# One ones-matmul group for two units: VectorE sums pairs of softmax weight tiles in the graph attention of a GNN stack

## The chip, the cores and the metric

The kernel runs on one core of a Trainium2 chip. The metric is the device time of one execution, in microseconds. Kernels are compared by medians of several executions.

## What is computed

A stack of four graph layers on 3125 nodes of 256 features with 50000 edges, each with a residual: a GIN layer with two batch norms, a GCN layer with two convolutions, a normalised sum over neighbours, and a two-level graph attention (GAT). The change lies in the attention's first level, which has four heads:

```python
h = (x @ W).reshape(N, H, C)
al_s = jnp.einsum('nhc,hc->nh', h, a_src)
al_d = jnp.einsum('nhc,hc->nh', h, a_dst)
e = jax.nn.leaky_relu(al_s[src] + al_d[dst], NEG_SLOPE)
m = jax.ops.segment_max(e, dst, num_segments=N)
ex = jnp.exp(e - m[dst])
denom = jax.ops.segment_sum(ex, dst, num_segments=N)
alpha = ex / denom[dst]
out = jax.ops.segment_sum(h[src] * alpha[:, :, None], dst, num_segments=N)
```

The kernel holds the edges as a dense matrix of counts `ct_d`, source nodes by destination nodes. For a head, `ex` is then a dense matrix of weights, zero where there is no edge. `out` is the feature rows times this matrix, and `denom` are its column sums.

## The kernel before

Nodes come in 25 blocks of Q = 125 (`NB = 25`). Destination nodes are split into two halves of 13 and 12 blocks (`HALF`, `COLS` = 1625 and 1500 columns). A step k of the attention is one head and one half: steps 0 to 7 are the four heads of the first level, k even the half of 13 blocks, k odd that of 12; steps 8 and 9 are the second level. A step has 25 units, one for each block j of source nodes; q = 25 k + j numbers the units.

One unit passes through the engines like this:

- SyncE loads the unit's counts into one of six buffers (`LC`).
- VectorE, `score` (L2458): the logits of the unit into the tile `TT[q % TR]`, one of a ring of TR = 4 tiles in R. It waits until TensorE has finished unit q - 4 (`l3_pe`) and until a DMA that reads the same tile has landed (`den_sum`).
- ScalarE, `exp_unit` (L1667): the exponential in place.
- VectorE, `weights` (L2471): times the counts, in place, then `l3_t` is raised. Ahead of it, in steps 0 to 5, one `max_unit` for the next head (L2242, for j = 0 L2239).
- TensorE, `unit` (L1402): waits for `l3_t`, then multiplies the features of the block with the weights, two groups of 128 features by the chunks of 500 columns (and one of 125), accumulating over the 25 units in PSUM banks 0 to 6. An fp32 matmul shows as two instructions in the trace: a unit of 13 blocks has 16, one of 12 blocks 12.
- The denominators of steps 0 to 5 (`DPE` = 6) are made in two parts. The first 1000 columns: TensorE, four matmuls of 250 columns against a block of ones, into four groups of 32 partitions of bank 6 (L1409, eight instructions a unit). The rest, 625 or 500 columns: POOL adds the tile's end to a DRAM tensor with accumulating DMAs (`den_sum`, L884), one chain for even and one for odd units. In steps 6 to 9 VectorE adds whole tiles instead (`den_add`, L2434) and there are no ones matmuls.

VectorE's order is written out in `attention`: score(q + 2), then den_add(q - 1) where there is one, then weights(q) with its maximum, then `beside(q)`. That is `results_in(q)` in steps 0 to 7: small results of the step before. TensorE makes one of them after each unit from j = 2 on (`result`): the transposed column maxima (L1302, L1309), the denominators (L1342, L1347), rows of their inverses (L1356) and the projections by W31 (L1366); a step of 13 blocks leaves 18 results, one of 12 leaves 14. VectorE reads them two units of its own later (j - 2 - LATER): L2330 to L2348, L2376 and L2377, L2387, L2397 with L2400. All go through PSUM bank 7: `aux_bank` lets TensorE write result i + 1 only after `aux_free` says that VectorE has read result i. In step 0 there is `late_max` as well: six more maxima, beside units 0, 1, 3, 5, 7 and 9 (`HELD`, L2242 on wA).

At the end of a step ScalarE takes the sums out of PSUM (`evac_step`, L1680, L1686).

`PT` is a buffer of 2000 columns; from column 1000 on it holds the second part of the denominators (`den_back`) and `denQ`. `denB` lies in wB and serves as denominators in steps 7 and 9.

Of the kernel before, what the change touches and what calls it, by code (L numbers as in the profile page):

```python
# [5 lines left out]
ALU = mybir.AluOpType  # L6
# [11 lines left out]
Q = 125  # L18
NB = N // Q
# [67 lines left out]
TR = 4  # L87
# [43 lines left out]
def gnn_stack(nc, x, src, dst, edge_weight, eps0, W01, b01, g01, be01, W02, b02, g02, be02,  # L131
              W11, b11, W12, b12, Wl1, bl1, root_idx, W2, b2, W31, as31, ad31, b31, gnw, gnb, gnms,
              W32, as32, ad32, b32, out):
    with ExitStack() as ctx:
        sems = {}

        def S(name):
            if name not in sems:
                sems[name] = ctx.enter_context(nc.semaphore(name))
            return sems[name]  # L140

        def sb(name, shape, dt=F32):
            return ctx.enter_context(nc.sbuf_tensor(name, shape, dt))
# [26 lines left out]
        PT = sb("PT", [128, 4 * 4 * Q])  # L170
# [41 lines left out]
        TT = [R[:, s * LW:(s + 1) * LW] for s in range(TR)]  # L212
# [18 lines left out]
        denB = wB[:, CT * NYC * 6:CT * NYC * 6 + COLS[1]]  # L231
# [102 lines left out]
        def lc_at(q):  # L334

            return MET + q + sum(a < q for a in HELD)
# [99 lines left out]
        for g_ in range(len(CB) + 1):  # L436
            if g_ < len(CB):
                HW_SEQ += [("turn", g_, k) for k in range(KT)]
            if g_:
                j, nj = CB[g_ - 1]  # L440
# [15 lines left out]
        def bank_of(f, c):  # L456
            return (f * 3 + c, 0) if c < 3 else (6, f * Q)
# [16 lines left out]
        PRE = [len(MGROUPS[0]) + 1, len(MGROUPS[1]) + 1]  # L474
# [11 lines left out]
        DPE = STEPS - 2  # L486
# [6 lines left out]
        def sum_count(q):  # L493

            k, j = divmod(q, NB)
            return (NB // 2 if j % 2 else NB - NB // 2) * k + j // 2
        denQ = PT[:, LW:LW + 3 * Q]

        def den_span(k):

            return (0, 0) if k < DPE else (0, COLS[k % 2])

        def den_adds(q):

            k, j = divmod(q, NB)
            return sum(NB for i in range(k) if den_span(i)[1]) + (j if k < STEPS + 2 and den_span(k)[1] else 0)


        EVS = [7, 6]
        ev0 = [sum(EVS[i % 2] for i in range(k)) for k in range(STEPS + 3)]  # L510
# [410 lines left out]
        def _(pe):  # L921
# [95 lines left out]
            for n, (what, g, x_) in enumerate(HW_SEQ):  # L1017
                j, nj = CB[g]
# [3 lines left out]
                else:  # L1022
                    done = HW_SEQ.index(("turn", g, KT - 1)) + 1
                    pe.wait_ge(S("ring_ev"), base["hw"] + done)
                    for m in range(hw_blocks(g, x_)):
                        o = (x_ + m - j) * Q
                        for k in range(KT):
                            last = mm(ps[0:Q, n % 4, m * D:(m + 1) * D], HT[:, g % 2, k, o:o + Q], w01[:, k, :],
                                      start=k == 0, stop=k == KT - 1)
# [216 lines left out]
            for q in range(LAYERS * NB):  # L1246
                step_unit(q)
                k, j = divmod(q, NB)
# [140 lines left out]
            def unit(q, rows):  # L1389
                k, j = divmod(q, NB)  # L1390
                half = k % 2
                pe.wait_ge(S("l3_t"), q + 1)
                for f in range(KT):
                    for c, (o, w) in enumerate(CHUNKS[half]):
                        bank, at = bank_of(f, c)
                        if j == 0 and k not in (0, STEPS) and bank < 6:
                            pe.wait_ge(S("agg_ev"), ev0[k - 1] + bank + 1)
                        if j == 0 and bank == 6 and f == 0 and 0 < k <= DPE:
                            pe.wait_ge(S("den_out"), k)
                        if j == 0 and bank == 6 and f == 0:  # L1400
                            pe.wait_ge(S("aux_free"), PRE[0] if k == 0 else aux0[k - 1] if k < STEPS else pre2 + PRE[0])
                        last = mm(ps[:, bank, at:at + w], rows[0:Q, j, f * 128:(f + 1) * 128], TT[q % TR][0:Q, o:o + w],  # L1402
                                  start=j == 0 and at == 0, stop=j == NB - 1, skip_group_check=c == 3)
                if k < DPE:
                    if j == 0 and k:
                        pe.wait_ge(S("den_out"), k)
                    nb, first, at = DQ[half]
                    for c in range(4):
                        last = mm(ps[c * 32:(c + 1) * 32, 6, at:at + nb * Q], ones[0:Q, 0:32],  # L1409
                                  TT[q % TR][0:Q, c * nb * Q:(c + 1) * nb * Q],  # L1410
                                  start=j == 0 and first == 1, stop=j == NB - 1, skip_group_check=True)
                last.then_inc(S("l3_pe"), 1)

            pe.wait_ge(S("ln_done"), 4 * NB + HALF[0][1])
# [21 lines left out]
            n = 0  # L1436
# [295 lines left out]
        def _(dve):  # L1732
            v_ = nc.vector
            tt, ts, stt, cp = v_.tensor_tensor, v_.tensor_scalar, v_.scalar_tensor_tensor, v_.tensor_copy
# [158 lines left out]
            for i, (g, part) in enumerate(PUNITS):  # L1893
                j0, nb = PG[g]
# [8 lines left out]
                for c, (o, w) in enumerate(LCHUNKS):  # L1903
                    for k in range(KT):
                        n = 4 * i + c * KT + k
# [330 lines left out]
            def max_unit(t, dst, score, first, done, name):  # L2236

                if first:
                    ts(dst, t, score, None, ALU.min).then_inc(S(name), 1)  # L2239
                else:  # L2240
                    dve.wait_ge(S(name), done)
                    stt(dst, t, score, dst, ALU.min, ALU.max).then_inc(S(name), 1)  # L2242
# [7 lines left out]
            for q in range(LAYERS * NB):  # L2250
                k, j = divmod(q, NB)
# [190 lines left out]
            def score(q):  # L2442

                k, j = divmod(q, NB)
                half, w = k % 2, COLS[k % 2]
                u = UV[k // STEPS][half]
                s8 = asc[0:Q, 1, (k // 2) * NB + j:(k // 2) * NB + j + 1] if k < STEPS else asb[0:Q, 1, j:j + 1]
                if q == 0:
                    dve.wait_ge(S("rows_clear"), 1)
                if q >= TR:  # L2450
                    dve.wait_ge(S("l3_pe"), q - TR + 1)
                    if q - TR < DPE * NB:
                        dve.wait_ge(S(f"den_sum{(q - TR) % NB % 2}"), 16 * (sum_count(q - TR) + 1))
                    if den_adds(q - TR + 1):
                        dve.wait_ge(S("l3_den"), den_adds(q - TR + 1))
                if j == 0:
                    dve.wait_ge(S(f"uv_in{half}"), 16 * (k // 2 + 1))
                stt(TT[q % TR][0:Q, 0:w], u[0:Q, 0:w], s8, u[0:Q, w:2 * w], ALU.add, ALU.max).then_inc(S("l3_a"), 1)  # L2458

            def weights(q):  # L2460

                k, j = divmod(q, NB)
                half, w = k % 2, COLS[k % 2]
                r = lc_at(q)
                t, lc = TT[q % TR][0:Q, 0:w], LC[r % LCR][0:Q, 0:w]
                dve.wait_ge(S(f"lc_in{r % LCR}"), 16 * (r // LCR + 1))
                if k < STEPS - 2:
                    max_unit(lc, macc[half][0:Q, :], asc[0:Q, 0, (k // 2 + 1) * NB + j:(k // 2 + 1) * NB + j + 1],
                             j == 0, len(EARLY) + lc_at(q - 1) + 1, "l3_max")
                dve.wait_ge(S("l3_exp"), q + 1)  # L2470
                stt(t, t, 1.0, lc, ALU.min, ALU.mult).then_inc(S("l3_t"), 1)  # L2471

            def attention(q0, q1, beside):

                score(q0)
                score(q0 + 1)
                for q in range(q0, q1):
                    if q + 2 < q1:
                        score(q + 2)
                    if q > q0:  # L2480
                        den_add(q - 1)
                    weights(q)
                    beside(q)
                den_add(q1 - 1)

# [27 lines left out]
            def norm_vectors(t0, t1, n):  # L2513
# [19 lines left out]
                tt(f[3], w[2], f[4], ALU.subtract).then_inc(S("gn_aff"), 1)  # L2533

            attention(0, STEPS * NB, results_in)
            norm_vectors(0, GT, 0)
            for i in range(results(STEPS - 1)):
# [80 lines left out]
```

## Time and profile before

| | us |
|---|---|
| median of 3 runs | 3499.51 |
| lowest, highest | 3499.39, 3502.76 |
| profiled execution | 3490.76 |
| its span | 3488.7 |
| TensorE busy | 3178.3 |
| VectorE busy | 2430.9 |
| L1402, TensorE, B features, x2800 | 1094.9 |
| L2471, VectorE, x250 | 444.8 |
| L2458, VectorE, first level, x200 | 368.9 |

The profile is of one execution. Times of groups are sums of durations; matmuls overlap, so that the starts of neighbouring ones say more than their durations. "Idle before" is the time in which the engine had nothing to do ahead of an instruction, and the releaser is what ended it.

### The profile page before, as it was taken

Reading aid. Unit: us, or ns where it says so; the run is one execution under the profiler, and the core shown is the slowest. Engines: PE = TensorE matmul, PEld = TensorE weight load, DVE = VectorE, ACT = ScalarE, POOL = GpSimd, SP = SyncE. Lnnn points to the kernel's source line nnn. Section 1 sums busy time; section 2 is a strip of 40 time slices with the busy share of each in tenths; the row PEclk is TensorE's granted clock in tenths of the full one; section 3 lists DMA queues with packets and bytes.
Section 4 is the critical chain, followed back from the end, with each engine's and each line's share of the span. In section 5 each row is a group of like instructions: output and inputs, shape, how many; then the busy total and the mean of one; then the engine's idle time right before and its main releaser. Section 6 shows DMA issues by size and latency. Waiting matters only on the chain.

```text
span 3488.7 us, 34571 instructions
## 1 busy us (share of the span) xinstructions
PE 3178.3 (91%) x12587; PEld 1842.6 (53%) x12587; DVE 2430.9 (70%) x3261; ACT 859.4 (25%) x1133; POOL 834.7 (24%) x710
## 2 busy tenths in 40 slices
PE   5679986987999999999499999999999999996998
PEld 4567764764545455587344444444444444473444
DVE  9972322346356553246898888888888898888987
ACT  1013322335000001143222222222222222252322
POOL 7888888840000000011011112211111000020000
PEclk6559998998999999999699999999999999998999
DMA  9999997993555553545466557655555422283422
GB/s 324 364 327 289 309 264 199 297 250 97 185 174 173 179 178 120 175 153 165 149 163 143 133 124 153 136 128 125 135 118 128 108 88 69 85 315 124 129 62 68
DMA packets 290916, 602.34 MB, mean 173 GB/s; under 512 B 94028, under 2 KB 161168, under 8 KB 288699
## 3 DMA queue, kind: packets, MB, share of 16 engines
q1 hardware_dynamic: 147995, 452.89, 40.4%
q0 software_dynamic: 90272, 87.23, 14.7%
q10 hardware_dynamic: 52480, 60.01, 5.8%
q8 instruction: 100, 1.64, 0.2%
q14 instruction: 69, 0.57, 0.0%
HBM read 385.57 MB, written 214.46 MB: 172 GB/s over the span
## 4 chain that ended last, share of the span: by engine, by line
PE 63%; DMA 10%; issue 9%; DVE 9%; POOL 6%; POOLq 2%; ACT 1%; ACTq 0%; DVEq 0%; SPq 0%
PE ps L1402 31%; PE ps L1234 15%; DMA pairs<-w 8%; POOL pairs L828 6%; PE ps L1203 4%; PE ps L1366 3%; PE ps L1409 2%; PE ps L1431 2%; DVE R L2471 2%; PE ps L1151 2%; DVE wB L2434 1%; PE ps L1045 1%; DVE PT L2242 1%; POOLq L818 1%; POOLq L813 1%
## 5 line engine op out<-in xcount | busy, mean ns | idle before, releaser
L1402 PE MATMUL ps<-R,B 125*128 125x500 f32 x2800 | 1094.9, 542 | 24.2 <-DVE R L2471 18.2
L1402 PEld LDWEIGHTS ps<-R,B 125*128 125x128 f32 x2800 | 504.1, 190 | 587.7 <-issue 552.8
L828 POOL DMA_INDIRECT pairs<-w x392 | 605.6, 1545 | 130.2 <-issue 105.7
L1667 ACT ACTIVATE R<-R,asc 125x1625 f32<-125x1625 f32 (+1 forms) x200 | 320.2, 1601 | 959.0 <-DVE R L2458 959.0
L2458 DVE SCALAR_TENSOR_TENSOR R<-H,asc 125x1625 f32<-125x1625 f32 (+1 forms) x200 | 368.9, 1845 | 133.8 <-PE ps L1409 110.6
L2471 DVE SCALAR_TENSOR_TENSOR R<-R 125x1625 f32<-125x1625 f32 (+1 forms) x250 | 444.8, 1779 | 0.0
L1045 PE MATMUL ps<-R,H 125*128 125x375 f32 (+1 forms) x1000 | 299.7, 446 | 51.0 <-DMA R<-pairs 50.5
L884 POOL DMA_DIRECT2D den_d<-R x138 | 118.3, 858 | 771.0 <-DVE R L2471 742.2
L1402 PE MATMUL ps<-R,H 125*128 125x500 f32 (+1 forms) x700 | 274.0, 547 | 19.2 <-DVE R L2471 17.5
L1234 PE MATMUL ps<-R,H 125*128 125x500 f32 (+1 forms) x700 | 275.0, 545 | 10.3 <-ACT H L1524 7.6
L1910 DVE TENSOR_TENSOR Fb<-Fb,ps 128x250 f32<-128x250 f32 (+1 forms) x140 | 67.2, 480 | 307.2 <-PE ps L1045 245.3
L1234 PE MATMUL ps<-R,B 125*128 125x500 f32 (+1 forms) x700 | 268.9, 540 | 1.6 <-ACT R L1608 0.9
L2242 DVE SCALAR_TENSOR_TENSOR Fb<-R,asc,Fb 125x1625 f32<-125x1625 uint16 (+1 forms) x144 | 265.0, 1840 | 0.0
L1045 PEld LDWEIGHTS ps<-R,H 125*128 125x128 f32 x1000 | 184.5, 192 | 126.4 <-DMA R<-pairs 51.1
L1402 PEld LDWEIGHTS ps<-R,H 125*128 125x128 f32 x700 | 125.9, 192 | 160.8 <-issue 131.2
L1234 PEld LDWEIGHTS ps<-R,H 125*128 125x128 f32 x700 | 127.8, 192 | 146.1 <-issue 141.6
L1234 PEld LDWEIGHTS ps<-R,B 125*128 125x128 f32 x700 | 126.0, 190 | 137.0 <-issue 136.1
L1065 PE MATMUL ps<-ident,R 125*125 125x125 f32 x1250 | 170.1, 284 | 22.2 <-ACT B L1564 14.2
L1791 DVE SCALAR_TENSOR_TENSOR R<-ps,Fb,R 128x512 bf16<-128x512 f32 (+3 forms) x392 | 190.1, 543 | 0.0
L1065 PEld LDWEIGHTS ps<-ident,R 125*125 125x125 f32 x1250 | 160.5, 195 | 42.6 <-ACT B L1564 18.9
L849 POOL DMA_DIRECT2D high_d<-Br x13 | 7.8, 601 | 640.5 <-DVEq L2173 640.3
L2097 DVE TENSOR_REDUCE R<-R 125x1 f32<-125x1625 uint16 (+1 forms) x50 | 88.9, 1778 | 101.3 <-DMA R<-ct_d 99.7
(370 smaller groups left out, 3437.4 us busy)
## 6 DMA issues: line engine op xcount, KB each, us to landing
pairs<-R SPq DMA_DIRECT2D x25, 3200.0 KB, 18.3
R<-ct_d SPq DMA_DIRECT2D x187, 406.2 KB, 3.6
R<-ct_d SPq DMA_DIRECT2D x187, 375.0 KB, 3.2
R<-pairs SPq DMA_DIRECT2D x25, 2500.0 KB, 11.7
R<-wt_d SPq DMA_DIRECT2D x50, 812.5 KB, 4.4
R<-wt_d SPq DMA_DIRECT2D x50, 750.0 KB, 4.2
den_d<-R POOLq DMA_DIRECT2D x75, 312.5 KB, 5.7
den_d<-R POOLq DMA_DIRECT2D x75, 250.0 KB, 4.7
```

What stands on the lines that cost most here:

```text
L828: pool.indirect_dma_start(pairs, bass.IndirectOffsetOnAxis(ap=key_u[:, c:c + 1], axis=0), val[:, c, :], None, compute_op=ALU.add)\
L884: pool.dma_start(den_d[a][k % 2], TT[q % TR][:, 8 * Q:w], accum_op=ALU.add).then_inc(S(f"den_sum{a}"), 16)
L1045: last = mm(ps[:, n % 4, 0:w], H[0:Q, j0 + m, k * 128:(k + 1) * 128], pair_rows_at(i)[0:Q, m, o:o + w, 0], start=m == 0, stop=m == nb - 1 ...
L1065: last = tr(ps[0:Q, 4 + 2 * (n % 2) + t, m * Q:(m + 1) * Q], pair_rows_at(i)[0:Q, m, b * Q:(b + 1) * Q, t], ident[0:Q, 0:Q])
L1203: last = mm(ps[:, bank, at:at + w], part[0:rows, jj, f * 128:(f + 1) * 128], TLr[u % TS][0:rows, o:o + w], start=j == 0 and i == 0 and at ...
L1234: last = mm(ps[:, bank, at:at + w], rows[0:Q, j, f * 128:(f + 1) * 128], TL[q % TS][0:Q, o:o + w], start=j == 0 and at == 0, stop=j == NB ...
L1402: last = mm(ps[:, bank, at:at + w], rows[0:Q, j, f * 128:(f + 1) * 128], TT[q % TR][0:Q, o:o + w], start=j == 0 and at == 0, stop=j == NB ...
L1667: a(t, t, ACT.Exp, bias=s2).then_inc(S("l3_exp"), 1)
L1791: stt(TW[c][:, b * CW + lo:(b + 1) * CW], ps[0:EP, (t % 2) * 2 + b, lo:CW], k, TRI[:, 0:CW - lo], ALU.is_equal, ALU.mult, accum_out=later[ ...
L2242: stt(dst, t, score, dst, ALU.min, ALU.max).then_inc(S(name), 1)
L2458: stt(TT[q % TR][0:Q, 0:w], u[0:Q, 0:w], s8, u[0:Q, w:2 * w], ALU.add, ALU.max).then_inc(S("l3_a"), 1)
L2471: stt(t, t, 1.0, lc, ALU.min, ALU.mult).then_inc(S("l3_t"), 1)
```

## The change

In steps 0 to 5 VectorE adds the weight tiles of units q - 1 and q, for every odd j, over the first 1000 columns, after weights(q) and ahead of `beside(q)`: `pair_sum`. The sum goes alternately into the first 1000 columns of PT and of denB (`PAIR`), and `l3_pair` is raised. TensorE leaves out the ones matmuls in even units, and in odd ones runs them on the sum, after the products and a wait for `l3_pair`. The last unit of a step, j = 24, has no partner and is summed alone as before. `pair_sums(q)` is the number of sums up to unit q. `pair_sum` waits for its own engine's weights (`l3_t`), for TensorE to have finished unit q - 4 (`l3_pe`), and once for the first five small results. `score` waits in addition for the sums that read the tile which it overwrites. The wait for `den_out` at the start of a step moves from j = 0 to j = 1. POOL's part of the denominators is unchanged.

```diff
--- before.py
+++ after.py
@@ -506,6 +506,13 @@
             return sum(NB for i in range(k) if den_span(i)[1]) + (j if k < STEPS + 2 and den_span(k)[1] else 0)
 
 
+        PAIR = [PT[:, 0:8 * Q], denB[:, 0:8 * Q]]
+
+        def pair_sums(q):
+
+            k, j = divmod(q, NB)
+            return min(k, DPE) * (NB // 2) + (min((j + 1) // 2, NB // 2) if k < DPE else 0)
+
         EVS = [7, 6]
         ev0 = [sum(EVS[i % 2] for i in range(k)) for k in range(STEPS + 3)]
 
@@ -1401,14 +1408,17 @@
                             pe.wait_ge(S("aux_free"), PRE[0] if k == 0 else aux0[k - 1] if k < STEPS else pre2 + PRE[0])
                         last = mm(ps[:, bank, at:at + w], rows[0:Q, j, f * 128:(f + 1) * 128], TT[q % TR][0:Q, o:o + w],
                                   start=j == 0 and at == 0, stop=j == NB - 1, skip_group_check=c == 3)
-                if k < DPE:
-                    if j == 0 and k:
+                if k < DPE and (j % 2 or j == NB - 1):
+                    if j == 1 and k:
                         pe.wait_ge(S("den_out"), k)
                     nb, first, at = DQ[half]
+                    if j % 2:
+                        pe.wait_ge(S("l3_pair"), pair_sums(q))
+                    t = PAIR[pair_sums(q) % 2] if j % 2 else TT[q % TR]
                     for c in range(4):
                         last = mm(ps[c * 32:(c + 1) * 32, 6, at:at + nb * Q], ones[0:Q, 0:32],
-                                  TT[q % TR][0:Q, c * nb * Q:(c + 1) * nb * Q],
-                                  start=j == 0 and first == 1, stop=j == NB - 1, skip_group_check=True)
+                                  t[0:Q, c * nb * Q:(c + 1) * nb * Q],
+                                  start=j == 1 and first == 1, stop=j == NB - 1, skip_group_check=True)
                 last.then_inc(S("l3_pe"), 1)
 
             pe.wait_ge(S("ln_done"), 4 * NB + HALF[0][1])
@@ -2451,6 +2461,8 @@
                     dve.wait_ge(S("l3_pe"), q - TR + 1)
                     if q - TR < DPE * NB:
                         dve.wait_ge(S(f"den_sum{(q - TR) % NB % 2}"), 16 * (sum_count(q - TR) + 1))
+                    if pair_sums(min(q - TR + 1, DPE * NB - 1)):
+                        dve.wait_ge(S("l3_pair"), pair_sums(min(q - TR + 1, DPE * NB - 1)))
                     if den_adds(q - TR + 1):
                         dve.wait_ge(S("l3_den"), den_adds(q - TR + 1))
                 if j == 0:
@@ -2470,6 +2482,20 @@
                 dve.wait_ge(S("l3_exp"), q + 1)
                 stt(t, t, 1.0, lc, ALU.min, ALU.mult).then_inc(S("l3_t"), 1)
 
+            def pair_sum(q):
+
+                k, j = divmod(q, NB)
+                if k >= DPE or j % 2 == 0:
+                    return
+                n = pair_sums(q)
+                if q >= 4:
+                    dve.wait_ge(S("l3_pe"), q - 3)
+                dve.wait_ge(S("l3_t"), q + 1)
+                if n == 1:
+                    dve.wait_ge(S("aux_full"), PRE[0])
+                tt(PAIR[n % 2][0:Q, :], TT[(q - 1) % TR][0:Q, 0:8 * Q], TT[q % TR][0:Q, 0:8 * Q], ALU.add)\
+                    .then_inc(S("l3_pair"), 1)
+
             def attention(q0, q1, beside):
 
                 score(q0)
@@ -2480,6 +2506,7 @@
                     if q > q0:
                         den_add(q - 1)
                     weights(q)
+                    pair_sum(q)
                     beside(q)
                 den_add(q1 - 1)
```

## Rows read from the trace of the kernel before

**Rows 1.** The page, parts 1 and 4: busy time; chain that ended last
```profile
PE 3178.3 (91%) x12587; PEld 1842.6 (53%) x12587; DVE 2430.9 (70%) x3261; ACT 859.4 (25%) x1133; POOL 834.7 (24%) x710
...
PE 63%; DMA 10%; issue 9%; DVE 9%; POOL 6%; POOLq 2%; ACT 1%; ACTq 0%; DVEq 0%; SPq 0%
```

**Rows 2.** Windows by step: length, busy by engine, then clock, DMA share, GB/s
```profile
1750.98:1914.00 163.02, 160.21 (x614) 76.16 (x614) 148.91 (x91) 41.69 (x27) 21.33 (x26) 0.98 0.66 158
1914.00:2075.36 161.36, 159.85 (x572) 68.16 (x572) 141.19 (x108) 42.38 (x34) 23.02 (x28) 1.00 0.54 124
...
sum 989.62, PE 979.29 PEld 444.34 DVE 868.20 ACT 256.96 POOL 155.14; mean PE 163.22 PEld 74.06 DVE 144.70 ACT 42.83 POOL 25.86
```

**Rows 3.** Waits of VectorE, 1750 to 2741: total us, times, longest us
```profile
DVE R L2458 <- PE ps L1409: 110.6, 133, 2.1
DVE R L2458 <- DMA den_d<-R: 3.0, 3, 1.6
```

**Rows 4.** Timeline of VectorE, a plain unit of 13 blocks: start, duration, instruction
```profile
2202.25 1.91 DVE L2458 SCALAR_TENSOR_TENSOR R<-H,asc 125x1625 f32<-125x1625 f32 x1 [0.75 <-PE ps L1409]
2204.08 1.91 DVE L2242 SCALAR_TENSOR_TENSOR Fb<-R,asc,Fb 125x1625 f32<-125x1625 uint16 x1
```

**Rows 5.** Chain that ended last, two plain units: start, us, what
```profile
2201.62 0.56 PE ps L1409 x8
2202.18 5.67 PE ps L1402 x16
...
2051.38 5.24 PE ps L1402 x12
```

**Rows 6.** Start of step 0: window, timeline of VectorE and TensorE
```profile
1750.98:1817.10 66.12, 65.11 (x240) 30.49 (x240) 64.57 (x37) 16.51 (x10) 7.97 (x10) 0.96 0.66 165
...
1771.49 1.77 DVE L2242 SCALAR_TENSOR_TENSOR wA<-R,asc,wA 125x1500 f32<-125x1500 uint16 x1
1773.18 1.90 DVE L2458 SCALAR_TENSOR_TENSOR R<-H,asc 125x1625 f32<-125x1625 f32 x1
...
1778.59 1.90 DVE L2458 SCALAR_TENSOR_TENSOR R<-H,asc 125x1625 f32<-125x1625 f32 x1
...
1817.10 1.10 PE L1402 MATMUL ps<-R,B 125*128 125x500 f32 x2 [0.58 <-DVE R L2471]
```

**Rows 7.** A denominator row of step 1: timeline of VectorE, chain
```profile
1969.77 1.78 DVE L2458 SCALAR_TENSOR_TENSOR R<-H,asc 125x1500 f32<-125x1500 f32 x1 [1.82 <-PE ps L1409]
...
1974.79 0.67 DVE L2387 COPY wA<-ps 128x500 f32<-128x500 f32 x1
...
1975.88 0.57 PE ps L1356 x4
```

**Rows 8.** A projection of step 1: timeline of VectorE, chain
```profile
2006.64 0.67 DVE L2397 TENSOR_TENSOR Fb<-ps,wA 128x500 f32<-128x500 f32 x1
2007.45 0.68 DVE L2400 BATCH_NORM_STATS2 wB<-Fb 128x6 f32<-128x500 f32 x1
...
2009.02 1.87 PE ps L1366 x4
```

**Rows 9.** Waits of TensorE's weight loads, 1750 to 2741: total us, times, longest
```profile
PEld ps L1302 <- DVE mcol L2330: 6.0, 15, 0.4
```

**Rows 10.** Timeline of TensorE, plain units of steps 6 and 7
```profile
2845.84 50.61 PE L1402 MATMUL ps<-R,B 125*128 125x500 f32 x144
...
3001.64 41.30 PE L1402 MATMUL ps<-R,B 125*128 125x500 f32 x96 [0.16 <-DVE R L2471]
```

**Rows 11.** Line L2434, VectorE: durations in ns min/median/max, first and last start
```profile
L2434 DVE TENSOR_TENSOR wB<-wB,R x48: 1708/1714/1722, 2904.2 to 3459.7; 125x1500 f32<-125x1500 f32 x48
L2434 DVE TENSOR_TENSOR X<-X,R x24: 1842/1844/1847, 2748.3 to 2892.5; 125x1625 f32<-125x1625 f32 x24
```

**Rows 12.** Timeline of VectorE, operations that wait for each other, step 3
```profile
2288.16 0.29 DVE L2336 TENSOR_SCALAR mcol<-mcol,kb 125x13 f32<-125x13 f32 x1
2288.49 0.18 DVE L2337 TENSOR_TENSOR mcol<-mcol,ald 125x13 f32<-125x13 f32 x1
```

## The prediction

> **What bounds the kernel now.** I read the page first. TensorE is busy for 91% of the span, VectorE for 70%, and the chain that ended last is TensorE's for 63% [rows 1]. The change lies in steps 0 to 5 of the heads, so I cut these from the trace: six stretches, 1750.98 to 2740.60, 989.6 us together; in them TensorE is busy 98 to 99% at a granted clock of 0.98 to 1.00, VectorE 88% [rows 2]. (Steps 0 and 1 and the sum of the six stand there; 3 and 5 are like 1, while 2 and 4 have some 172 us.). The waits of VectorE say how the two are coupled: its score (L2458) waits 110.6 us in 133 pieces for TensorE's L1409, and next to nothing else [rows 3]. VectorE is thus the follower, by some 0.75 us a unit, the time that it waits ahead of a plain score [rows 4]. A plain unit of 13 blocks takes TensorE 5.68 us for the products and 0.56 us for the ones matmuls, 6.24 together, and one of 12 blocks 5.24 and 0.56, 5.80 together [rows 5]. The granted clock of nearly 1 is the level of 2.4 GHz.
>
> Two places are tighter than this. The first is the start of step 0, where VectorE has six more maxima to take (L2242 on wA, in the units of HELD). There it has no idle time ahead of its scores, and TensorE waits for it [rows 6]. The second is the hand-over of the small results. They all go through bank 7, and TensorE may write result i+1 only when VectorE has read result i (`aux_free`). With a denominator row of a 12-block step, VectorE's copy ends at 1974.79 + 0.67 = 1975.46, and TensorE goes to the next row at 1975.88 [rows 7]: 0.42 us of play. With a projection the product ends at 2006.64 + 0.67 = 2007.31 and TensorE comes at 2009.02: 1.71 us [rows 8]. That TensorE's weight loads wait for such a read already, 15 times for the maxima (L1302), never over 0.4 us, says that this play is nearly used up [rows 9].
>
> **What the change removes.** 12 of 25 units in each of 6 steps lose their four ones matmuls: 72. The row says 0.56 us each; but step 6, which has none, does nine plain 13-block units back to back in 50.61 us, 5.62 each, and step 7 eight 12-block ones in 41.30, 5.16 each [rows 10]. So what goes is 6.24 - 5.62 = 0.62 and, with 5.20 for the short unit (between this 5.16 and the 5.24 of above), 0.60. Together 36 x 0.62 + 36 x 0.60 = 44 us of TensorE's work. The group's mean of 386 ns is not the price: eight such instructions lie within 0.56 us.
>
> **What it adds.** 72 sums of 1000 columns on VectorE. The same addition takes 1844 ns for 1625 columns and 1714 for 1500, 1.04 ns a column; from either it is 1194 for 1000 [rows 11]. It adds the unit's own weights, just written, and waits for them (`l3_t`). Between operations that don't wait for each other the next starts some 0.08 us before the former's end: scores of 1.91 us are followed 1.83 us later [rows 4]. Here this overlap is lost, and a gap comes on top. A waiting operation starts 0.04 us after the end of the one before (2288.16 + 0.29 to 2288.49), or 0.14 with a semaphore instruction in between (2006.64 + 0.67 to 2007.45) [rows 8, 12]. I take 0.05, nearest to the first, since nothing but waits is between. One sum thus costs 0.08 + 0.05 + 1.194 - 0.08 (the operation behind it overlaps) = 1.24 us; its bounds are 1.11 (nothing exposed) and 1.33 (a gap of 0.14). 72 of them are 89 us, beside 110.6 us of idle time. By totals they fit. Pair by pair they don't.
>
> The Trainium skill, in VectorE: DVE Perf Modes, section The DRAIN you can't avoid, says that the pipe empties after every operation in any case and that a semaphore costs nothing extra. The rows show the contrary: an operation of 1.91 us is followed 0.08 before its end where nothing waits, and one of 0.29 us 0.04 after its end where something does. By that rule of the Trainium skill the sum would cost the lower bound, 1.11; what that gives is a rival below.
>
> The other edits cost nothing. The wait for `l3_pe` at q-3 is one that the score of two units on has made already. TensorE's wait for `l3_pair` stands behind 5.68 or 5.24 us of products that start when the weights are ready, and the sum is there 1.24 us after them. The two buffers are reused four units later, the waits in `score` for sums that VectorE issued earlier itself are past. The accumulating DMAs of POOL (L884) cost VectorE 3.0 us in all [rows 3]; their room, from weights to the score four units on, becomes 5.4 + 1.24 = 6.7 us instead of 6.2 (6.3 instead of 5.8 in the short steps), so they gain some. Queued behind the sum on VectorE are the next score, which has its 0.75 us, and `beside(q)`, the reading of a result, which has 0.42.
>
> **The sum.** I walk the 150 units with three rules. VectorE starts score(q+2) when it is free and TensorE has ended unit q-2 (0.1 us later), then does the maximum, the weights, in odd units the sum, and the result; a 13-block unit is 5.41 us of it (score to score, 1773.18 to 1778.59) and a 12-block one 5.02 (score to copy, 1969.77 to 1974.79) [rows 6, 7]. TensorE starts unit q 0.05 us after its weights, and result i+1 0.05 us after result i was read. Durations are those above. For the kernel before the walk gives 161.9, 161.3, 171.1, 161.3, 171.1, 161.3 for the six steps, 988.0 in all; the trace has 163.0 and 161.4 for the first two and 989.6 in all [rows 2]. With the change:
> - Step 0, first ten units: VectorE needs 10 x 5.41, six maxima of 1.69 (1771.49 to 1773.18 [rows 6]) and 5 x 1.24, 70.4 us; the walk had 65.5 (trace: 66.1 [rows 6]). +5.0. The next four +0.1.
> - Plain pairs: VectorE 2 x 5.41 + 1.24 = 12.06 against 12.48 before (TensorE would be 11.86). -0.42 each; in a short step 11.28 against 11.60, -0.32. VectorE is now the later one. The last eleven units of step 0 give -1.7, the last nine of steps 2 and 4 -1.8 each.
> - Pairs with denominator rows: VectorE reads 1.24 us later, TensorE comes 0.60 earlier, play 0.42: TensorE waits some 1.5 us at bank 7, and the pair takes about 0.9 longer. The column maxima, the inverse and the first rows of a short step come to +0.7 +1.2 +0.6, those of steps 2 and 4 to +0.6 +0.5 +0.9.
> - Pairs with projections: 1.24 + 0.60 - 1.71, some 0.2 us of wait. In the middle of the run -0.35 a pair, but the first pays +0.9; six units come to +0.2 (short) and +0.1 (long).
> - First pair of a step -0.6 (units before it ran ahead); last units of a short step -0.3 and +0.1.
>
> By step: +3.3; +2.0 three times in 1, 3, 5; -0.3 twice in 2 and 4. Together 3.3 + 6.0 - 0.6 = +8.7 us: all 44 us of TensorE's savings are given back, and somewhat more. Steps 6 and 7 and what follows don't change. The profiled execution took 3490.76 us (span 3488.7), which becomes 3499.5; the median of the runs was 8.75 above it, 3499.51, and becomes 3508.2. With the bounds of a sum, 1.11 and 1.33, the walk gives -0.1 and +15.0; an error of 0.04 us in TensorE's saving per unit moves it by 3.5.
>
> **Rivals.**
> 1. Nothing is exposed between weights and sum (1.11 us each). Then VectorE's pace is 11.93 a plain long pair and the waits at bank 7 are 0.13 shorter; the walk gives -0.1 us, 3499.4. (That is how the rule of the Trainium skill, VectorE: DVE Perf Modes, The DRAIN you can't avoid, would have it.) Against it stand the chains of [rows 12]. 0.15; what lies between it and my case, below +7, has another 0.18.
> 2. The result hand-over isn't a constraint, since the reads have more play than the two places show; then only VectorE's own pace counts. The walk without that rule gives +3.3 in step 0, -2.4 in each short and -5.0 in each long step: -13.9, 3485.6. For it speaks that no wait at this place is now over 0.4; against it that there are 15 [rows 9], and the code's wait. It decides by the play at the read: over 1.8 us and the rival holds. 0.08.
> 3. The totals hold: 89 us go into 110.6 us of idle time, and all 44 us of TensorE come off: 3455.5. A ring of four tiles (TR) would have to carry 1.24 us from odd to even units and through the result stretches; in plain pairs alone VectorE's 12.06 is above 11.86. 0.03.
> 4. The short pauses of TensorE lower its granted clock. In step 0's first 66 us it had such pauses, one of 0.58 us, at 0.96 [rows 6], and the steps as they are run at 0.98 to 1.00 [rows 2], so I don't expect it; a twentieth of step 0 at half clock would be +8 us more, inside my upper end.
>
> **How the numbers follow.** Slower is the forecast, with 0.56 for the case of the sum from +7 up: 3508 us. The range 3494 to 3517 has the exposed and unexposed sum with the saving's error at both ends and half of rival 2. A change of 0.2% (7 us) is about what a measurement of this kernel can tell from none. Faster than that: rivals 2 and 3, 0.11. Within: 0.15 + 0.18 = 0.33. Slower: 0.56.
>
> **What would show it.** VectorE's new group at L2496 or thereabouts, 72 of 1194 ns, starting some 0.05 us after the end of the weights; L1409 with 624 instead of 1200 instructions; the wait of L2458 for L1409 down from 110.6 to below 40; TensorE waiting for L2387, L2330 and L2397 for some tens of us in all, pieces of up to 1.5 us; the first ten units of step 0 at about 70.5 us instead of 66.1. I am wrong if the steps 1, 3, 5 are below 161, or if TensorE's waits at results stay small.

## The result, and the profile after

The changed kernel takes 3519.9 us in the median of its runs (3518.8 to 3525.0), against 3499.5 us for the kernel before in the same session: the ratio is 1.0062, with a 95% interval of 1.0051 to 1.0074. It is 20.4 us slower, beyond the upper end of the range, 3517. The profile is that of the run of 3519.42 us.

The page of the changed kernel, parts 1 and 5: busy time by engine, and the scores' group with its count, busy time, mean ns and the idle time ahead of it.

```profile
PE 3152.6 (90%) x12011; PEld 1840.0 (52%) x12011; DVE 2510.8 (71%) x3333; ACT 859.5 (24%) x1133; POOL 834.6 (24%) x710
...
L2470 DVE SCALAR_TENSOR_TENSOR R<-H,asc 125x1625 f32<-125x1625 f32 (+1 forms) x200 | 368.4, 1843 | 68.2 <-PE ps L1419 40.5
```

The sums, from the groups of VectorE by line and shape, 1740 to 3090 us, with the same columns:

```profile
L2496 DVE TENSOR_TENSOR PT<-R 125x1000 f32<-125x1000 f32 x36 | 43.2, 1201 | 4.0 <-DVE R L2483 0.5
```

TensorE has 576 instructions fewer than in [rows 1], 72 times 8; VectorE has 72 more. So the change does what it says. Its windows by step, cut at ScalarE's first eviction of each step as in [rows 2]: length, busy time of TensorE, its weight loads, VectorE, ScalarE and POOL, then clock, DMA share, GB/s.

```profile
1756.91:1924.12 167.21, 152.54 (x517) 73.67 (x517) 161.92 (x102) 40.96 (x26) 20.73 (x25) 0.98 0.64 154
1924.12:2090.60 166.48, 154.88 (x475) 67.14 (x475) 154.66 (x119) 42.37 (x33) 22.48 (x28) 0.99 0.52 120
2090.60:2262.86 172.26, 162.67 (x563) 79.56 (x563) 161.74 (x113) 44.08 (x32) 45.49 (x53) 1.00 0.69 146
...
sum 1010.29, PE 942.35 PEld 434.24 DVE 948.41 ACT 256.23 POOL 155.45; mean PE 157.06 PEld 72.37 DVE 158.07 ACT 42.70 POOL 25.91
```

The six steps take 1010.3 us instead of 989 (the two first windows of before end 0.7 us off an eviction; cut at the evictions they are 162.3, 161.4, 171.3, 161.4, 171.3 and 161.4, 988.9 in all). The steps gained 4.9, 5.1, 1.0, 4.8, 1.0 and 4.6 us, 21.4 together: the whole of the difference between the medians. The two profiled executions differ by more, 28.7 us, and 5.9 of it lies ahead of step 0, which begins at 1756.91 instead of 1750.98 us, in code that the change doesn't touch. TensorE's busy time fell from 979.3 to 942.4, by 37 us, and still it took longer: it waits. VectorE's waits for the ones matmuls fell from 110.6 to 40.5 us; in their place TensorE waits for VectorE. The waits of VectorE and of TensorE's matmuls between 1750 and 2768 us: total, times, longest.

```profile
DVE R L2470 <- PE ps L1419: 40.5, 39, 2.4
...
PE ps L1409 <- DVE R L2483: 38.6, 25, 17.9
PE ps L1309 <- DVE mcol L2340: 12.3, 12, 1.2
PE ps L1316 <- DVEq L2351: 9.0, 6, 2.6
PE ps L1363 <- DVE wA L2397: 7.4, 5, 1.5
PE ps L1373 <- DVE wA L2397: 7.2, 5, 1.5
```

The first of TensorE's lines holds 17.9 us ahead of the first unit, which the kernel before has too (16.8); what is left of it is mostly step 0. There the first ten units take 70.6 us (1756.91 to 1827.48), where the prediction had about 70.5. The other four are the hand-over of small results. Of such waits the kernel before had only one kind at its matmuls, ahead of its L1309 (L1316 of the changed kernel), 4.3 us in 6, longest 0.7; at its weight loads none was over 0.4 us [rows 9]. Here is one, a denominator row of step 1, in VectorE's timeline (start, duration, instruction, idle time ahead of it and what ended it):

```profile
1993.42 1.71 DVE L2483 SCALAR_TENSOR_TENSOR R<-R 125x1500 f32<-125x1500 f32 x1
1995.24 1.20 DVE L2496 TENSOR_TENSOR PT<-R 125x1000 f32<-125x1000 f32 x1
1996.35 0.67 DVE L2397 COPY wA<-ps 128x500 f32<-128x500 f32 x1
```

and in TensorE's:

```profile
1990.37 5.21 PE L1409 MATMUL ps<-R,B 125*128 125x500 f32 x12
1997.08 0.64 PE L1363 MATMUL ps<-ident,dcol 125*128 125x125 f32 x4 [1.50 <-DVE wA L2397]
```

TensorE comes 0.6 us sooner, since the even unit has no ones matmuls, and finds bank 7 unread, since the sum stands ahead of the copy. This is the 1.5 us that the prediction had worked out from [rows 7].

Three things were not in it. The first two are about the sum itself. A sum at the start of step 0, a later one behind which a score follows, and the weights ahead of each, from VectorE's timeline:

```profile
1775.84 1.84 DVE L2483 SCALAR_TENSOR_TENSOR R<-R 125x1625 f32<-125x1625 f32 x1
1777.72 1.20 DVE L2496 TENSOR_TENSOR PT<-R 125x1000 f32<-125x1000 f32 x1
...
2223.23 1.85 DVE L2483 SCALAR_TENSOR_TENSOR R<-R 125x1625 f32<-125x1625 f32 x1
2225.18 1.20 DVE L2496 TENSOR_TENSOR PT<-R 125x1000 f32<-125x1000 f32 x1
2226.52 1.91 DVE L2470 SCALAR_TENSOR_TENSOR R<-H,asc 125x1625 f32<-125x1625 f32 x1
```

The first starts 0.04 us after the weights' end (1775.84 + 1.84), the second, which waits for `l3_pe` as well, 0.10 (2223.23 + 1.85). And the score starts 0.14 us after the sum's end, where a small result starts 0.09 before it (1995.24 + 1.20 to 1996.35 above). So in a plain pair a sum costs not 1.24 but 2226.52 - 2223.23 = 3.29 us less the 1.77 from weights to score without it, 1.52 us.

The third is the clock. The last column maxima of step 1 and the unit behind them, timeline of TensorE:

```profile
1969.21 0.27 PE L1316 MATMUL ps<-ident,uvc 125*26 125x125 f32 x1 [2.58 <-DVEq L2351]
1969.32 6.89 PE L1409 MATMUL ps<-R,B 125*128 125x500 f32 x12
```

Two windows, up to the pause's end and behind it, with the clock as the third number from the right:

```profile
1961.22:1969.21 7.99, 5.42 (x17) 2.33 (x14) 7.41 (x10) 1.55 (x1) 0.84 (x1) 1.00 0.56 126
1969.21:1976.14 6.93, 6.93 (x14) 2.83 (x14) 5.29 (x4) 1.54 (x1) 0.85 (x1) 0.75 0.29 46
```

TensorE waited 2.58 us for the five small operations behind the sum and the last maxima. The unit after the pause took 6.89 us instead of 5.2, at a mean granted clock of 0.75: half of that window at 1.2 GHz, half at 2.4. Below, this is called a stretch at half clock. The same stands in steps 3 and 5, and nowhere in steps 1 to 5 of the kernel before. That is 1.7 us three times.

### The profile page after: what moved, and what is told of

Read it like the earlier page. It is cut to its first block and busy times, and to the rows that moved or that the text cites. A ratio compares the mean times of both kernels' runs of the same rounds, so it can differ in the third digit from the quotient of the medians.

```text
span 3517.3 us, 33578 instructions
## 1 busy us (share of the span) xinstructions
PE 3152.6 (90%) x12011; PEld 1840.0 (52%) x12011; DVE 2510.8 (71%) x3333; ACT 859.5 (24%) x1133; POOL 834.6 (24%) x710
## 5 line engine op out<-in xcount | busy, mean ns | idle before, releaser
L2470 DVE SCALAR_TENSOR_TENSOR R<-H,asc 125x1625 f32<-125x1625 f32 (+1 forms) x200 | 368.4, 1843 | 68.2 <-PE ps L1419 40.5
L1409 PEld LDWEIGHTS ps<-R,H 125*128 125x128 f32 x700 | 126.2, 192 | 160.9 <-issue 131.4
L1072 PE MATMUL ps<-ident,R 125*125 125x125 f32 x1250 | 172.7, 287 | 27.6 <-ACT B L1574 16.3
```

Source lines behind the costliest of these rows:

```text
L1072: last = tr(ps[0:Q, 4 + 2 * (n % 2) + t, m * Q:(m + 1) * Q], pair_rows_at(i)[0:Q, m, b * Q:(b + 1) * Q, t], ident[0:Q, 0:Q])
```

## The experiments

The walk of the prediction was first repaired by what the profile shows: 1.20 us for a sum and 0.10 ahead of it (+12.5 us instead of +8.7), the score waiting 0.13 behind it (+16.3), and 1.7 us for each of the three pauses of over 2.3 us (+21.4). By step it gives +4.8, 4.7, 1.1, 4.7, 1.1, 4.7, against the measured 4.9, 5.1, 1.0, 4.8, 1.0, 4.6. A walk that is fitted to one profile proves little, so each experiment's steps were worked out with it ahead of the run. Theory A below is this walk.

**The small result ahead of the sum.**

```diff
                     weights(q)
-                    pair_sum(q)
                     beside(q)
+                    pair_sum(q)
```

> One edit to the changed kernel: in every unit VectorE reads the small result (beside) first and makes the sum of the pair after it. The number of sums, matmuls and waits stays. Theory A (the sum delays the reading of the small results, TensorE waits for them at bank 7, and one of these waits lets its clock fall): steps 1, 3 and 5 become some 5.9 us shorter than in the changed kernel (166.5 to 160.6 by the evictions), steps 2 and 4 some 3.9, step 0 the same; 25 us in all, so 3495 us, 4 us below the kernel before. TensorE's pause ahead of L1316 in steps 1, 3, 5 falls from 2.58 us to under 1.5 and the long unit of 6.9 us behind it is gone. Rival B (VectorE is the slower engine and each sum costs its 1.3 us wherever it stands): no change, 3520 us; the score then always waits for the sum, which would even add some 0.2 us for each of the 40 sums that have a result behind them, 3528.

Measured: 3495.5 us, ratio to before 0.999 (0.998 to 1.000). Swapping two lines takes away 24 us. Steps 160.1, 168.1, 161.2, 168.0, 160.9 for 1 to 5, step 0 unchanged at 167.8. The rival that VectorE's total sets the pace falls: it has the same operations. TensorE's waits at the small results, all their lines together, fell from 42.6 to 24.2 us. There is still one stretch at half clock, in step 3 from 2307.4 us on, behind a pause of 0.83 us at L1349.

**One unit only.**

```diff
-                    pair_sum(q)
+                    late = q // NB % 2 and q % NB == 7
+                    if not late:
+                        pair_sum(q)
                     beside(q)
+                    if late:
+                        pair_sum(q)
```

> One edit to the changed kernel: only in unit j = 7 of steps 1, 3 and 5 VectorE reads the small result (the last column maxima, which TensorE needs for L1316) ahead of the sum; everywhere else the order is as changed. Theory A: the pause of 2.58 us ahead of L1316 shrinks to about 1.4, the unit behind it takes 5.2 us instead of 6.9 because the granted clock stays at its upper level, and each of the three steps becomes 2.2 us shorter (1.7 of it the clock); 6.8 us in all, 3513 us. Rival B (the 6.9 us unit has another cause, such as the DMAs around it): the unit stays at 6.9 us, and the steps lose at most 0.6 us each, 3518 us.

Measured: 3513.1 us, the time that was expected, but not in the way expected. TensorE in step 1:

```profile
1962.47 0.27 PE L1316 MATMUL ps<-ident,uvc 125*26 125x125 f32 x1 [1.27 <-DVEq L2351]
1962.58 5.20 PE L1409 MATMUL ps<-R,B 125*128 125x500 f32 x12
...
1969.17 1.25 PE L1349 MATMUL ps<-ones,PT 125*125 125x1 f32 x10 [0.84 <-DVE ag L2358]
...
1970.59 6.90 PE L1409 MATMUL ps<-R,B 125*128 125x500 f32 x12
```

The pause fell to 1.27 us and the unit behind it takes 5.20; but the next pause, of 0.84 us, now has a stretch at half clock behind it. Steps 1, 3 and 5 became only about 1 us shorter each, and step 4 had such a stretch too (173.9 us). The six steps are 1009.6 us, against 1010.3 in the changed kernel; the lower median isn't explained by them. Of the 8.5 us by which its profiled execution is shorter, 5.9 lie ahead of step 0 (it begins at 1751.01 us), where the two kernels don't differ. So this run shows where the pause comes from, but not that removing it saves the clock's 1.7 us.

**Useless work in the pause.**

```diff
+                if n in (2, 4, 6):
+                    for i in range(3):
+                        mm(ps[:, 7, 256:506], w31[:, 0, 0:128], w31[:, 1, 0:250], start=True, stop=True,
+                           skip_group_check=True)
                 pe.wait_ge(S("uv_made"), n + 1)
```

> The changed kernel, with three matmuls of 250 columns more ahead of L1316 in steps 1, 3 and 5, into columns of bank 7 that nobody reads, once the last maxima are read and before the wait for uv_made: some 1.3 us of useless work in TensorE's pause of 2.58 us, of which about 1.3 us stay idle. Nothing that VectorE does changes. Theory A (the unit of 6.9 us behind the pause is the clock's, and it is the pause that lets the clock fall): no stretch at half clock behind L1316, that unit takes 5.2 us, and each of the three steps becomes 1.7 us shorter, 164.4 us; 5 us in all, 3515 us. Rival E (the clock falls by the sum of the pauses at the small results around it, 0.9, 1.2, 2.6 us, not by this one): the stretch at half clock comes all the same, there or a unit or two later, as it did when the pause was 1.27 us, and the steps stay at 166 us.

Measured: 3522.7 us (ratio to before 1.0072, 1.0052 to 1.0091). In step 1:

```profile
1971.38 1.53 PE L1317 MATMUL ps<-w 128*128 128x250 f32 x6 [1.38 <-DVE mcol L2344]
1972.75 0.27 PE L1320 MATMUL ps<-ident,uvc 125*26 125x125 f32 x1
1972.86 5.20 PE L1413 MATMUL ps<-R,B 125*128 125x500 f32 x12
```

In all three steps the unit behind takes 5.2 us, with no stretch at half clock there; steps 1 and 3 are 1.5 us shorter than in the changed kernel, 165.0 and 164.6. It is one profile, but three places of three: at this place it is TensorE's being idle for 2.58 us that lets the clock fall. But in this run step 4 had a stretch at half clock behind a pause of 1.33 us, and in step 5 VectorE's queue stood still once for 1.5 us, with a pause of TensorE of 2.82 us and a stretch at half clock behind it. No gain is left in the total, and both theories have a part: the long pause is the surest to lower the clock, and shorter ones do it now and then.

**The changed kernel again.**

> The changed kernel once more, unchanged, for a second profile: which of its steps have a stretch at half clock again. Theory A: steps 0 to 5 at 167.2, 166, 172.3, 166, 172.3, 166 us, with three stretches behind L1316 of steps 1, 3, 5 or, by how the phases fall, one missing (1.7 us less in that step), as in the run without the l3_pe wait.

3520.0 us; steps 168.4, 166.4, 174.0, 166.1, 172.3, 166.2. The three stretches at half clock are there again, and a fourth in step 2 (2139.3 us), behind a pause of 1.35 us. In the run without the `l3_pe` wait, which follows, step 3 had the pause of 2.51 us and no such stretch: 163.7 us, against 165.4 in steps 1 and 5.

**No second wait ahead of the sum.**

```diff
                 n = pair_sums(q)
-                if q >= 4:
-                    dve.wait_ge(S("l3_pe"), q - 3)
                 dve.wait_ge(S("l3_t"), q + 1)
```

> One edit to the changed kernel: pair_sum no longer waits for l3_pe at q - 3, which the score two units on has waited for already. Theory A (a second wait ahead of the sum adds to the gap behind the weights: it is 0.04 us in the first two sums, which have no such wait, and 0.10 in the others): the sum starts 0.04 us after the weights' end everywhere, 0.06 us earlier, and the steps get 0.6 to 0.7 us shorter each, 4.2 us in all, 3516 us. Rival B (the gap has to do with how busy the engine's queue is, not with the wait): the gap stays 0.10 us and the time 3520 us.

Measured: 3515.8 us, 4.1 less. VectorE:

```profile
2225.64 1.84 DVE L2483 SCALAR_TENSOR_TENSOR R<-R 125x1625 f32<-125x1625 f32 x1
2227.52 1.20 DVE L2494 TENSOR_TENSOR PT<-R 125x1000 f32<-125x1000 f32 x1
```

The gap is 0.04 us, and long steps are 0.75 us shorter. A wait that has long been met, ahead of one that hasn't, costs 0.06 us here. Over all the sums the idle time ahead of them falls from 7.7 to 2.4 us, 0.07 a sum.

**The two halves of the change by themselves.**

```diff
# VectorE's half: sums as changed, TensorE's ones matmuls as before
-                if k < DPE and (j % 2 or j == NB - 1):
+                if k < DPE:
...
# TensorE's half: no pair_sum(q), no waits for l3_pair
-                    t = PAIR[pair_sums(q) % 2] if j % 2 else TT[q % TR]
+                    t = TT[q % TR]
```

> VectorE's half of the change alone: it makes the 72 sums, and TensorE goes on with its ones matmuls in every unit, on the single tiles, as in the kernel before. Theory A (a sum of 1.3 us does not fit into VectorE's 0.75 us ahead of a score, nor into the play of the small results): steps 0 to 5 become longer by 6.1, 4.8, 3.6, 4.8, 3.6, 4.8 us, 28 in all (3527 us), and 3 to 5 more if TensorE's clock falls as in the changed kernel. Rival C (89 to 95 us of sums go into 110 us of VectorE's idle time): below 5 us.

> TensorE's half of the change alone: the ones matmuls are left out in even units, and in odd ones they run on the unit's own weights; VectorE makes no sums. It leaves the even units' weights (but for j = 24) out of the first 1000 denominators. Theory A (72 times 0.61 us are on TensorE's path, less what the small results' hand-over takes back): step 0 4.8 us, steps 1, 3, 5 5.5, steps 2 and 4 6.5 below the kernel before, 34.5 in all, 3465 us. Rival B (the ones matmuls run beside something else and cost little): under 10 us.

Measured: the sums alone 3525.2 us (1.0064, 1.0047 to 1.0080), six steps 1018.8, 29.9 us above before, of which one stretch at half clock; by the medians it is 24.5. TensorE's half alone 3468.0 us (0.990, 0.9883 to 0.9916), six steps 953.8, 35.1 below, and 32.8 by the medians. The walk had 28 and 34.5. The saving is real; the sums cost as much as they do where they stand. Together they would be -5.2 if they added up; the changed kernel is at +21.4. The two meet at bank 7: one makes TensorE arrive earlier, the other makes VectorE read later. With the read ahead of the sum, the first experiment, the six steps are 986.0, 2.9 below before and thus near -5.2. How much of the 26.6 us between is bank 7, and how much comes from plain pairs, where TensorE's shorter pair leaves VectorE's as the longer one, wasn't separated.

**Another order on VectorE.**

```diff
                     weights(q)
-                    pair_sum(q)
+                    if q < 10:
+                        next_max(q)
                     beside(q)
+                    pair_sum(q)
+                    if q >= 10:
+                        next_max(q)
```

`next_max` is the `max_unit` of `weights`, which stood ahead of the weights. `pair_sum` has no wait for `l3_pe` here, as in the run without it; that alone was worth 4.1 us.

> The changed kernel with VectorE's order in a unit turned round from unit 10 on: weights, small result, sum, and the maximum for the next head last (it was maximum, weights, sum, small result); units 0 to 9 have weights, maximum, small result, sum. The wait for l3_pe ahead of the sum is left out too. The same operations, all of them. Theory A (what costs is where the sum stands in the chain from TensorE's unit over the score and the weights to the small result, not VectorE's total): weights and small results come 1.8 us earlier, the score no longer waits for the sum, TensorE is the bound again outside step 0: steps 1, 3, 5 at 155 us, 2 and 4 at 163.7, step 0 some 2.5 above the kernel before; 31.6 us below the kernel before in all, 3468 us. Rival B (each sum costs its 1.3 us as VectorE is the slower engine): a plain pair of 13 blocks stays at 12.1 to 12.3 us, the steps 1, 3, 5 are not under 160, and the time is 3510 us or more.

Measured: 3464.7 us, ratio 0.991 (0.9889 to 0.9932). Steps 1 and 2 in its windows, with the columns as above:

```profile
1923.17:2078.10 154.93, 151.61 (x475) 66.88 (x475) 152.68 (x119) 42.40 (x33) 21.98 (x27) 1.00 0.62 131
2078.10:2241.63 163.53, 161.44 (x563) 79.32 (x563) 160.56 (x115) 44.12 (x33) 45.58 (x53) 1.00 0.81 153
```

A plain pair in its VectorE timeline:

```profile
2202.81 1.84 DVE L2480 SCALAR_TENSOR_TENSOR R<-R 125x1625 f32<-125x1625 f32 x1
2204.69 1.20 DVE L2501 TENSOR_TENSOR PT<-R 125x1000 f32<-125x1000 f32 x1
2205.80 1.91 DVE L2252 SCALAR_TENSOR_TENSOR Fb<-R,asc,Fb 125x1625 f32<-125x1625 uint16 x1
```

Both engines are now busy for 98% of these steps. The same operations that cost 21 us in one order gain 31.5 us over the six steps in another; the walk had 31.6. Not all of that is the change's, as the next run shows. The maximum stands where the score used to wait for the sum, and TensorE gets its weights 1.8 us earlier.

**The order without the change.**

> A control: the kernel before, without sums and with all its ones matmuls, but with VectorE's order of the faster experiment: weights, small result, maximum (units 0 to 9: weights, maximum, small result). Theory A (before the change TensorE is the bound nearly everywhere, so the order is worth little): 4.5 us below the kernel before, mostly at L1316, where TensorE waits for the column maxima, 3495 us. Rival D (what made the reordered kernel faster is the order by itself and not the sums in their new place): 20 us or more.

Measured: 3491.6 us, ratio 0.9975 (0.9964 to 0.9986), six steps 982.1. The order alone is worth 6.8 us there (9.1 by the medians), 3.0 of it in step 0, more than the 4.5 expected and far from the 34.5 by which the reordered kernel with sums is faster. In this order, then, the change itself is worth 24.7 us over the six steps (982.1 to 957.4), and that includes both of its halves: what TensorE saves, less what the sums cost.

**No pairs in units 0 to 9.**

```diff
-                if k >= DPE or j % 2 == 0:
+                if k >= DPE or j % 2 == 0 or q < 10:
```

with TensorE's ones matmuls in every unit there, and `pair_sums` counting five fewer.

> The reordered kernel with sums (weights, small result, sum, maximum, no l3_pe wait ahead of the sum), and in units 0 to 9, where VectorE has six more maxima to take, no pairs: TensorE runs its ones matmuls there in every unit on the single tiles. Theory A: step 0 gets 6.6 us shorter than in the reordered kernel, since VectorE is the bound in these ten units and loses five sums; the rest stays; 3458 us. Rival B (the ten units are bound by TensorE's low clock or by its own work): no gain, or some 3 us more for the five ones groups that come back.

Measured: 3459.7 us, ratio 0.9876 (0.986 to 0.9893), 41 us faster than before. Step 0 is 159.0 us instead of 164.9, the rest within 0.5 a step; six steps 951.8, 37.1 below before. The first ten units take 65.35 us instead of 70.02. The reordered kernel had two stretches at half clock in them, at 1787.0 and 1814.3 us, which are gone as well; whether they cost anything where VectorE sets the pace isn't shown. This is the fastest kernel of the study: the change, with the sum put where VectorE has the room for it.

Not tried: the kernel with the score's wait for the sum left out. Without it the score may overwrite a tile that the sum still reads. Its price, 0.2 us where a score stands right behind a sum, is read from the timelines alone.

## Why the prediction was wrong

The direction and the mechanism were right, the size was not: 8.7 us were worked out where 20.4 came.

- What bounds: right. VectorE follows by 0.75 us, start of step 0 and bank 7 are the tight places. TensorE waited there 1.50 us where some 1.5 was worked out.
- What is removed: right. 44 us of TensorE's work; 35 of them on the path when TensorE's half is taken alone, where the walk had 34.5. The first ten units of step 0 came out as predicted, 70.6 for 70.5 us.
- The addition: 1194 ns were read from [rows 11], 1201 came. Right.
- The gap ahead of it: 0.05 was taken, as only waits stand between. There are two waits, and 0.10 came. This and the 7 ns cost 3.8 us by the walk. The term lay within its bounds, but the sentence that the wait for `l3_pe` costs nothing was wrong: without it the kernel is 4.1 us faster.
- "The waits in `score` for sums that VectorE issued earlier itself are past." This step failed. `score(q)` waits for `pair_sums(q - TR + 1)`. For the score right behind the sum of unit q that is `pair_sums(q + 3 - 4 + 1)`, the sum just issued. Reading the index would have shown it. It costs some 0.2 us (2226.52 - 2225.18 = 1.34, less the 1.11 to a small result) where no small result stands between, and 3.8 us in all by the walk. The price of a sum in a plain pair, 1.52 us, was above the bound of 1.33.
- The clock: this step failed too, and it is the largest term, 5.1 us that the sum put at nothing. Rival 4 was set aside because short pauses seemed not to lower it, and the 0.96 of step 0's start was read together with a pause of 0.58 us. That reading was wrong. The half clock stands in the first 5.0 us, behind the 16.8 us in which TensorE waited ahead of the first unit, and nothing is lost after them. Windows of the kernel before, with the clock as the third number from the right:

```profile
1750.98:1756.00 5.02, 5.01 (x6) 2.19 (x7) 5.02 (x3) 1.52 (x1) 0.54 (x1) 0.50 0.75 215
1756.00:1817.10 61.10, 60.09 (x235) 28.30 (x233) 59.55 (x35) 14.99 (x10) 7.42 (x9) 1.00 0.66 161
```

  The pause that mattered is the one at L1316 in steps 1, 3 and 5, which was not looked at. The kernel before had 0.71 us there; with the prediction's own 1.24 for the sum and 0.60 for the even unit that makes 2.55, and 2.58 came. In step 0, where the prediction expected pauses to count, TensorE paused for 1.9 to 2.0 us four times in the first ten units, without a fall.
- Rival 1, nothing exposed behind a wait: fell. The rule of the Trainium skill (VectorE: DVE Perf Modes, The DRAIN you can't avoid), that a semaphore costs nothing extra, does not hold here: the next operation starts 0.09 us before the end without a wait, 0.04 after it with one, 0.10 with two.
- Rival 2, no constraint at the hand-over: fell by the run with the small result ahead of the sum, which only swaps the read and the sum and takes 24 us away. Some 3.4 of them are two stretches at half clock fewer.
- Rival 3, the totals: fell as stated. But the last run comes to -41 us by the medians, -37 in the six steps, where it had -44. Some 7 of that the order gives without the change. The room was there; the order didn't let the sums into it.

By terms: 8.7 as predicted, 3.8 for gap and duration, 3.8 for the score's wait, 5.1 for the clock, 21.4 in all, and 21.4 measured over the six steps. The exact agreement is in part fitting and luck: the last three terms were put in with this profile in view. The second profile of the same kernel, with a fourth stretch at half clock, has 1013.3 us in the six steps, 24.4 above before. The clock's term is shown in place, by the useless work in the pause, but not as a total, since these stretches come and go from run to run.

## What to carry to other kernels

When work moves from a bound engine to one with idle time, don't compare totals: follow what stands behind the new work on its engine, and who waits for that, and count the earlier arrival of the relieved engine too. Add these up at each hand-over to find the longest pause, and ask what a pause of that length does to TensorE's clock. Try the place before the verdict: here the six steps with the same 72 additions are 21 us longer than before with the sum ahead of a read that another engine waits for, and 31.5 us shorter with it behind that read and the next maximum moved to the room it leaves (6.8 of that without the additions, by the order alone). For each wait in the code, put in the numbers and see which instruction it means; "earlier" may be the one just ahead.

## What the runs showed of the hardware

- An operation of VectorE that waits for the engine's own last operation loses the overlap of 0.08 us and starts 0.04 us after its end; a second wait ahead of it, though met long before, costs 0.06 to 0.07 us more.
- In these runs a pause of TensorE of 2.5 us or more within the six steps was followed by a stretch at half clock, 1.7 us lost, in nine cases of ten (the tenth is step 3 without the `l3_pe` wait); pauses of 0.8 to 2.05 us were so now and then. The sums alone had three pauses of 2.02 us at L1316, the same place, and one stretch behind them. The Trainium skill (TensorE: Matmul & The Clock Gate, A second HAM failure mode: psum-queue depth-cycling) tells, for a bf16 kernel, of short idle spells between groups of matmuls, frequent enough to make the clock swing between its levels. The stretches here, 1.7 us lost each, are of that kind, though in fp32 and behind single pauses.
